# Graph kernel, first relation layer: tiny count products issued between the large sums of a group instead of in one run behind them

## What is computed

```python
h = node_feat @ W_emb + b_emb
for l in range(2):
    W = jnp.einsum('rb,bdf->rdf', w_coe[l], bases[l])
    T = jnp.einsum('nd,rdf->rnf', h, W)
    msg = T[etype, src] * norm
    agg = jax.ops.segment_sum(msg, dst, num_segments=N)
    h = agg + h @ self_loop[l]
    ... # batch norm, relu
```

## Time and profile before

| | us |
|---|---|
| median of 3 runs | 6612.25 (6593.21 to 6656.78) |
| the profiled execution's own time | 6709.38 |
| its span, first to last instruction | 6707.6 |
| the stage with L756, first to last start | 236.9 to 3740.9 |
| TensorE matmul busy, whole span | 4545.6 (68%) |
| VectorE busy, whole span | 3830.7 (57%) |
| ScalarE busy, whole span | 2425.1 (36%) |
| GpSimd busy, whole span | 2436.6 (36%) |

### The profile page before, as it was taken

One profiled execution on the slowest core, in us unless ns is written; L12 is line 12 of the kernel. 1 busy time (PEld: TensorE's weight loads), 2 busy tenths in 40 slices (PEclk: granted clock), 3 DMA queues, 4 the chain that ended last, 5 costly groups with the idle time before them and its releaser, 6 DMA issues. The chain is left out here.

```text
span 6707.6 us, 157901 instructions
## 1 busy us (share of the span) xinstructions
PE 4545.6 (68%) x54120; PEld 3396.8 (51%) x54121; DVE 3830.7 (57%) x8330; ACT 2425.1 (36%) x3822; POOL 2436.6 (36%) x2046
## 2 busy tenths in 40 slices
PE   5465655656555555555655499999989466666778
PEld 2244444444444444444444366666645266666767
DVE  4155555554455544545545566666630689999843
ACT  2123333233233223223223366666610145555600
POOL 0444544444444444444444000000000067777700
PEclk8677777777777777777777699999989778888889
DMA  5444444444444444444444422222258234444378
GB/s 201 132 123 138 146 142 136 134 138 138 134 135 137 133 127 137 134 129 142 138 128 146 137 77 77 80 77 76 80 193 284 74 148 153 153 153 153 105 249 259
DMA packets 673171, 935.65 MB, mean 139 GB/s; under 512 B 150771, under 2 KB 567006, under 8 KB 666174
## 3 DMA queue, kind: packets, MB, share of 16 engines
q1 hardware_dynamic: 470114, 548.86, 25.7%
q10 hardware_dynamic: 146524, 270.11, 10.9%
q0 software_dynamic: 56448, 115.72, 6.9%
HBM read 653.23 MB, written 281.17 MB: 139 GB/s over the span
## 5 line engine op out<-in xcount | busy, mean ns | idle before, releaser
L643 POOL DMA_INDIRECT f_rows<-table,f_recs x1715 | 1652.8, 964 | 1960.1 <-DMA f_recs<-edge_records 1162.4
L756 PE MATMUL f_acc<-f_rows,f_hot 128*128 128x264 f32 x3430 | 1181.9, 509 | 368.3 <-issue 295.4
L756 PEld LDWEIGHTS f_acc<-f_rows,f_hot 128*128 128x128 f32 x3430 | 848.5, 257 | 567.2 <-issue 351.9
L2013 PE MATMUL a_psum<-state_and_spare,a_weights 128*128 (+1 forms) x4802 | 662.4, 308 | 296.9 <-DVE a_weights L2131 152.4
L1963 POOL TENSOR_TENSOR a_weights<-a_powers,a_counts 128x896 f32<-128x896 f16 x245 | 719.6, 2945 | 336.9 <-ACT a_powers L2053 305.9
L2013 PEld LDWEIGHTS a_psum<-state_and_spare,a_weights 128*128 128x128 f32 x4802 | 651.6, 224 | 310.6 <-issue 203.8
L1224 ACT ACTIVATE g_grow<-g_gps 128x512 f16<-128x512 f32 x1225 | 667.1, 595 | 343.1 <-PE g_gps L1161 342.6
L816 ACT ACTIVATE f_counts_by_destination<-f_pm 128x896 f16<-128x896 f16 x343 | 314.7, 917 | 1085.3 <-PE f_pm L723 864.2
L705 PE MATMUL f_cnt<-f_dhot,state_and_spare 32*128 32x32 f16 x9604 | 238.4, 182 | 643.2 <-issue 642.7
L1181 PE MATMUL g_zps<-g_ohot,g_grow 32*128 32x256 f16 x19992 | 655.3, 269 | 0.7 <-issue 0.6
L1263 DVE TENSOR_SCALAR g_ohot<-count,slot_target 128x256 f16<-128x256 f16 x2499 | 537.1, 281 | 153.1 <-PE g_zps L1181 147.8
(11 more groups left out here) (272 smaller groups left out, 5923.7 us busy)
## 6 DMA issues: line engine op xcount, KB each, us to landing
f_rows<-in_edge_attr SPq DMA_DIRECT2D x343, 320.0 KB
g_srow<-slot_sources SPq DMA_DIRECT2D x245, 320.0 KB
counts_by_destination_f<-f_counts_by_destination ACTq DMA_DIRECT2D x343, 224.0 KB
no_edge_penalty<-f_pen ACTq DMA_DIRECT2D x343, 224.0 KB
s_ring<-counts_by_destination_f SPq DMA_DIRECT2D x98, 784.0 KB
a_pen<-no_edge_penalty SPq DMA_DIRECT2D x49, 1568.0 KB, 9.9
a_counts<-counts_by_source_f SPq DMA_DIRECT2D x49, 1568.0 KB, 6.7
e_ring<-counts_by_source_f SPq DMA_DIRECT2D x343, 224.0 KB, 3.8
```

The costliest lines, as they stand in the source:

```text
L643: e.indirect_dma_start(out=rows[:, j, 0:D], out_offset=None, in_=k.table_d[0], in_offset=bass.IndirectOffsetOnAxis(ap=recs[:, j, 4:5].bitc ...
L756: m = e.matmul(acc[:, 0:GW], hot[:, j, :], rows[:, j, :], start=j == 0, stop=j == SLOTS - 1)
L2013: m = e.matmul(psum[:, 4 + i // 3, i % 3 * (D + 4):i % 3 * (D + 4) + D + 1], weights[:, j, i * P:(i + 1) * P], k.msg[:, bass.ds(hb * SEG + ...
```

## The change

`count` is split into `begin_count` (the two waits and the 8 products of L700) and `count_cells` (the tiny ones). For tiles from 1 on, in groups 2 to 5, TensorE now does `begin_count` after the waits of the group and ahead of its first large product, and puts the tiny products of the block between the large ones: 3, 3, 3, 3 and 4 source tiles' worth (12, 12, 12, 12 and 16 products) behind the first to the fifth. `ring` is raised by the fifth large product as before, `counted` by the last tiny one. Ranking, transposes and the rest come behind. The last tile's counts, behind the loop, stay as they were. No instruction is added or removed, and no other engine's program changes.

```diff
-            def count(t, b):
+            def begin_count(t, b):
...
+            def count_cells(b, first_cell, end_cell):
+
+                lo, n = BLOCKS[b]
+                for j in range(first_cell, end_cell):
                     for u in range(QUARTERS):
                         q = slice(u * QW, (u + 1) * QW)
                         m = e.matmul(cnt[:, u, j * QW:(j + 1) * QW], shot[q, b % 2, j, :], dhot[q, lo + j, :],
                                      start=False, stop=j == n - 1)
-                m.then_inc(counted, 1)
+                return m
...
-                    for j in range(g * PER, (g + 1) * PER):
+                    b = g - 2
+                    between = 0 <= b < len(BLOCKS) and not first
+                    if between:
+                        begin_count(t - 1, b)
+                    for i in range(PER):
+                        j = g * PER + i
                         m = e.matmul(acc[:, 0:GW], hot[:, j, :], rows[:, j, :], start=j == 0, stop=j == SLOTS - 1)
-                    m.then_inc(ring, 1)
+                        if i == PER - 1:
+                            m.then_inc(ring, 1)
+                        n = BLOCKS[b][1] if between else 0
+                        part = range(i * n // PER, (i + 1) * n // PER)
+                        if len(part):
+                            c = count_cells(b, part.start, part.stop)
+                            if part.stop == n:
+                                c.then_inc(counted, 1)
...
-                        if 2 <= g < 2 + len(BLOCKS):
-                            count(t - 1, g - 2)
```

More of the change, by code:

```diff
@@ L701, in count @@
                                  start=i == 0, stop=False)
-                for j in range(n):
+            def count_cells(b, first_cell, end_cell):
+                lo, n = BLOCKS[b]
+                for j in range(first_cell, end_cell):
                     for u in range(QUARTERS):
@@ L706, in count @@
                                      start=False, stop=j == n - 1)
-                m.then_inc(counted, 1)
+                return m
+            def count(t, b):
+                begin_count(t, b)
+                count_cells(b, 0, BLOCKS[b][1]).then_inc(counted, 1)
             def turn_counts(t, g, final=False):
```

## The result

The changed kernel takes 7184.66 us (median of 4 runs, 7174.64 to 7194.2), the kernel before 6619.99 (4 runs on the same chip): ratio 1.0819, interval 1.0784 to 1.0854. Forecast were 6860 us and +3.7%. The profiled execution has a span of 7192.5 us at a mean granted clock of 0.77 (before: 6707.6 and 0.823).

The account below looks back on a forecast made before the run. A chain through waits bounds the kernel, with PE stalling while POOL gathers. Terms +12.7 - 9.4 + 2.1 = +5.4, say 5.2 us a tile over 48 tiles, 250 us: forecast 6860 us, range 6560 to 7190.

Parts of the forecast that it names:

- the wait goes ahead of the sums: PE's wait for cnt_moved loses its cover: +5.1 us in block 1, +2.9 block 2, +4.7 block 3, +12.7 a tile.
- crawl shortened: PE's stalls in the tiny products while POOL gathers: 3.1 us less in block 0, 6.3 in block 2, -9.4 a tile.
- alternation: Bare weight loads where PE changes between large and tiny products: bounds 0 and 4.2 us a tile, middle +2.1 taken.
- The sum stays at its 4.71 us: Block 3's large sum on PE keeps its low-clock length, twice the 2.44 us of the group before.
- The limited number: While POOL gathers, PE passes some 92 instructions, weight loads included, at full pace, then crawls until the run ends.
- I take the stalls as real: PE's 17 us a tile of stalls are not made by the profiler; otherwise unprofiled runs would be 833 us shorter.
- the stall goes wholly: Rival: PE's 17 us a tile are saved for 12.7 paid, -206 us, 6406 us; chance 0.14.
- the stalls stay: Rival: PE's stalls stay as long and only move, 14.8 us a tile, 710 us, 7320 us; chance 0.15.
- Instruction fetch: Rival: PE's stalls are pages of its program arriving, same price as 7320 us; inside the 0.15.
- POOL's run: Sign: POOL's longest run in a tile is 10 gathers instead of 15.
- ACT's distance: Sign: ACT's bank copies keep their distance of 5.4 us to the transposes.
- L700's wait: Sign: PE's idle time ahead of L700, released by ACT, grows from 2.7 to about 12 us a tile.

Follow-up runs that it names:

- plain transfers: Kernel before with POOL's indirect gathers replaced by same-size plain transfers: 5680.01 us, 0.8555; on another chip 5684.85 us, 0.998. Changed kernel likewise: 6666.47 us, 1.0037.
- one run behind: Changed kernel with its waits kept ahead, but all tiny products of a block in one piece after the fifth large product: 6929.12 us, 1.0431 times the kernel before.
- busy wait: Changed kernel plus 12 unread f32 products during each wait of blocks 1 to 3: 7006.56 us, 1.0432 times before; on another chip 6601.22 us, 1.1594.
- the milder orders: Changed kernel with only block 0 mixed: 0.9904 times before; all blocks begun ahead of the fourth large product: 0.9955; only blocks 0 and 2 so: 0.9862.

## Why the prediction was right or wrong

| term, us a tile | forecast | measured |
|---|---|---|
| the wait goes ahead of the sums | +12.7 | +13.6 (plain transfers, one run behind less before) |
| crawl shortened | -9.4 | -10.4 (gathers less plain: 21.1 before, 10.7 after) |
| alternation | +2.1 | +6.8 (plain transfers, mixed less one run behind) |
| sum | +5.4 | +10.0 |

The measured terms are differences between five kernels, taken so that they add up to the measured sum; that they do is no evidence of its own. With the gathers in place, mixing costs less: the changed kernel takes 5.0 us a tile more than the one run behind (82.0 and 77.0, on two chips).

**The wait for `cnt_moved`** was right in kind; that its size fits so well is partly luck. In groups 3 to 5 PE waits 5.2, 5.2 and 5.1 us, and idle time ahead of their L700 went to 15.5 us a tile from 3.6 (+11.9). With plain transfers all idle time rose by 10.0, and the other 3.6 us of the 13.6 are busy time in the same instructions at a lower clock (0.79 for 0.87 over the stage), behind waits in which PE idles. The forecast had 12.7 as idle time alone and nothing for the clock of blocks 1 and 2. The three large sums of the plain kernel with one run behind, and one of the three of the plain kernel before, which are alike:

```profile
2048.05 3.94 PE L767 MATMUL f_acc<-f_rows,f_hot 128*128 128x264 f32 x10
...
2060.38 4.60 PE L767 MATMUL f_acc<-f_rows,f_hot 128*128 128x264 f32 x10
...
2071.61 4.11 PE L767 MATMUL f_acc<-f_rows,f_hot 128*128 128x264 f32 x10
```

```profile
2030.28 2.44 PE L753 MATMUL f_acc<-f_rows,f_hot 128*128 128x264 f32 x10
```

With the gathers two of these three sums were slow before the change already (3.88 and 4.71 us), behind stalls. So the prediction's "The sum stays at its 4.71 us" holds for block 3, and the clock that it left out for block 2 (2.44 us there, 4.6 with one run behind) is small beside the 12.7.

**The crawl** was right too, also in its mechanism: a run of 10 gathers instead of 15, block 2 now free of it (5.6 us a tile before), a remainder in block 0 (2.4 for 8.8), and large sums hit as well (2056.13). The limited number holds over the trace before: in 89 of its 93 runs of 10 or more gathers (the first tile left out) PE stalls after 93 to 130 matmuls and weight loads, against the 92 that the prediction counted once. One sum in it has a slip: for block 0, 6.3 less 1.6 and 1.6 is 3.1 and not 3.7, so its own numbers give -8.8 for the term. "I take the stalls as real" holds: some 20 us a tile vanish when the gathers are plain.

**Alternation is the step that failed.** Its bounds, 0 and 4.2 us a tile, were worked out as bare weight loads at the durations of the earlier trace rows. For full clock this was sound: +1.1 us a block, 3.4 a tile. The Trainium skill, "TensorE: Matmul & The Clock Gate", section "The mechanism", has loads overlap only where row groups differ, which made 4.2; the full-clock periods agree with it better than with my middle of 2.1. What the term put at nothing is the clock: the mixed stretch often doesn't keep or reach the full level where the same work in two pure pieces does (sum of block 1 with one run behind: 3.94 us, then 64 tiny ones in 0.65). With gathers its mean clock in blocks 0 to 2 is 0.54, 0.52 and 0.53. The other 3.4 of the 6.8 us are what is left for this: the three mixed stretches take 5.4 us a tile more than the unmixed ones (18.0 and 12.6), and the rest is busy time in the work behind them. The upper bound was therefore none: it took a price per change and no price for the level of the clock. With 6.8 for 2.1 the sum would have been +10.1, against +10.0 measured.

**The rivals.** That the stall goes wholly is refuted: gathers still cost 10.7 us a tile, not 0. That the stalls stay (14.8 us a tile, 7320 us) is nearer to the time measured than my forecast, but for a reason that isn't its own; the stalls did shrink. Instruction fetch by itself is refuted by the plain transfers, under which the same program has no stall; a fetch that the gathers hold up is not. Of the signs named ahead, POOL's run, ACT's distance and L700's wait came out (10.3 us a tile with ACT as its releaser, for about 12); a tile of 76 to 79 us did not, nor did 5 to 8 us of idle time in the tiny products: it was 2.2, and only about 1 us of the crawl moved to large sums and keys.

**What stays open** is why the mixed stretch loses the clock with PE busy throughout. Idle waits ahead of it take part: work in them won 2.8 us a tile with plain transfers and 4.6 with gathers. But block 0 falls without any additional wait, and only in 26 of 46 tiles, with the same work ahead of it. No run here shows what decides.

## What to carry to other kernels

Before putting small work between large work of an engine, look at what the large work covered: here it hid 5 us of ACT's copies in each of three blocks, and the same edit with the wait left behind three of the five sums cost nothing. Mixing kinds of matmuls has two prices, one per change and one through the granted clock, and only the first can be read from weight loads; take the clock's lower level over the whole mixed stretch as the upper bound (here 6.93 us a block, 4.13 at full clock and 3.01 unmixed). And an unexplained "issue" idle that lines up with another engine's transfers is best settled by one run that replaces those transfers by plain ones: here it showed 14% of the kernel's time. It names the transfers, and not yet what they hold up.

## What was not expected of the hardware

The crawl depends on the chip. With real gathers and the same program, the kernel before took 5694.67 us on one of the five chips of the experiments and 6639 to 6725 on the other four; on the first, its plain version took 5684.85. In the kernel before it ends 2 to 3.8 us after the start of the last gather of a run in 120 of 132 stalls of the tiny products and the keys, and it hits SP too. In the kernel before, four loads of records took SP up to this long while gathers ran:

```profile
2100.65 10.53 SPq L620 DMA_DIRECT2D f_wrec<-edge_records  x4
```

The median of 46 such rows is 8.05 us. With plain transfers it is 3.97, and with gathers on the chip without the crawl (busy wait) 3.94. So it is not a limit of the matrix engine. On the chip without it the change costs 17% (with plain transfers; with the gathers it was not run there as it stands), on the others 8%: how much a shorter stall pays back depends on where the kernel runs. For the same reason the 1% that the milder orders won is not to be counted on: with plain transfers, block 0 alone mixed costs 3.5 us a tile.
